# A 128-step gated recurrence on one core: where the three gate sums are joined, and the order of VectorE's side work around place 7

## The reference, cut to what matters

```python
def step(h, inp):
    x_t, prop = inp
    comb = jnp.concatenate([x_t, h], axis=-1)
    z = jax.nn.sigmoid(comb @ Wz + bz)
    r = jax.nn.sigmoid(comb @ Wr + br)
    comb2 = jnp.concatenate([x_t, r * h], axis=-1)
    h_cand = jnp.tanh(comb2 @ Wh + bh)
    h_new = (1.0 - z) * h + z * h_cand
    h_next = jnp.where(prop, jnp.tanh(h_new @ Wp + bp), h_new)
    return (h_next, h_new)
# do_prop: every 4th step except the last; result: x + the h_new of all steps
```

## Time and profile before

| | busy us | share of the span | instructions |
|---|---|---|---|
| TensorE matmuls (PE) | 1033.4 | 99% | 20746 |
| weight loads (PEld) | 953.2 | 92% | 20746 |
| VectorE (DVE) | 880.9 | 85% | 2880 |
| ScalarE (ACT) | 777.0 | 75% | 1789 |

### The profile page before, as it was taken

One profiled execution on the slowest core, in us unless ns is written; L12 is line 12 of the kernel. 1 busy time (PEld: TensorE's weight loads), 2 busy tenths in 40 slices (PEclk: granted clock), 3 DMA queues, 4 the chain that ended last, 5 costly groups with the idle time before them and its releaser, 6 DMA issues.

```text
span 1038.9 us, 48087 instructions
## 1 busy us (share of the span) xinstructions
PE 1033.4 (99%) x20746; PEld 953.2 (92%) x20746; DVE 880.9 (85%) x2880; ACT 777.0 (75%) x1789; POOL 0.2 (0%) x4
## 2 busy tenths in 40 slices
PE   9999999999999999999999999999999999999998
PEld 4577999999999999999999999999999999999998
DVE  6978888898989899898989989989898998876666
ACT  6877777777878778777887777878777777665565
POOL 0000000000000000000000000000000000000000
PEclk9999999999999999999999999999999999999999
DMA  9312211001111011110011110111100100000001
GB/s 331 110 43 84 84 54 44 23 23 43 43 43 43 4 44 42 44 43 23 23 44 43 44 43 11 35 44 43 44 29 17 43 23 23 23 10 17 24 24 44
DMA packets 38484, 47.26 MB, mean 45 GB/s; under 512 B 2176, under 2 KB 34048, under 8 KB 37888
## 3 DMA queue, kind: packets, MB, share of 16 engines
q1 hardware_dynamic: 38000, 44.12, 12.6%
q10 hardware_dynamic: 272, 0.07, 0.0%
HBM read 27.40 MB, written 16.78 MB: 43 GB/s over the span
## 4 chain that ended last, share of the span: by engine, by line
PE 98%; DMA 1%; SPq 0%; DVE 0%; issue 0%; ACT 0%; DVEq 0%
PE acc L1360 38%; PE x_acc L1274 34%; PE acc L1368 17%; PE x_acc L1164 8%; DMA x_part<-wz_dram 1%; PE x_acc L1295 0%; SPq L419 0%; SPq L416 0%; DVE mag_win L982 0%; SPq L425 0%; SPq L424 0%; DVE x_lo L889 0%; PE acc L1170 0%; ACT gate L745 0%; DVE new L1099 0%
## 5 line engine op out<-in xcount | busy, mean ns | idle before, releaser
L1274 PE MATMUL x_acc<-x_hi,win_hi 128*128 128x256 f16 x1092 | 298.0, 273 | 0.0
L1274 PE MATMUL x_acc<-x_lo,win_hi 128*128 128x256 f16 x1092 | 297.9, 273 | 0.0
L1274 PE MATMUL x_acc<-x_hi,win_lo 128*128 128x256 f16 x1092 | 297.9, 273 | 0.0
L589 ACT ACTIVATE gate<-gate,unscale 128x128 f32<-128x128 f32 (+1 forms) x316 | 128.6, 432 | 136.4 <-DVE gate L1067 77.7
L595 ACT ACTIVATE gate<-acc,unscale 128x128 f32<-128x128 f32 (+1 forms) x384 | 123.8, 371 | 97.9 <-PE acc L1360 97.7
L1368 PE MATMUL acc<-h_split,wrec_hi 128*128 128x128 f16 x2704 | 178.8, 220 | 0.0
L1360 PE MATMUL acc<-h_split,wrec_lo 128*128 128x64 f16 x4096 | 177.5, 194 | 0.0
L1360 PE MATMUL acc<-q_split,wrec_hi 128*128 128x64 f16 x4000 | 162.2, 194 | 0.0
L555 ACT ACTIVATE x_part<-x_acc,bias,part_unscale 128x256 f32<-128x256 f32 x312 | 154.6, 561 | 6.4 <-PE x_acc L1274 5.5
L1360 PEld LDWEIGHTS acc<-h_split,wrec_lo 128*128 128x128 f16 x4096 | 154.2, 98 | 4.7
L1368 PEld LDWEIGHTS acc<-h_split,wrec_hi 128*128 128x128 f16 x2704 | 153.7, 98 | 0.0
(11 more groups left out here) (141 smaller groups left out, 1517.5 us busy)
## 6 DMA issues: line engine op xcount, KB each, us to landing
out_dram<-x_blk SPq DMA_DIRECT2D x30, 512.0 KB, 3.2
x_blk<-x_dram SPq DMA_DIRECT2D x24, 512.0 KB, 3.8
x_blk<-x_dram SPq DMA_DIRECT2D x3, 1024.0 KB, 8.7
x_part<-wz_dram SPq DMA_DIRECT2D x4, 256.0 KB, 6.8
x_part<-wh_dram SPq DMA_DIRECT2D x4, 256.0 KB, 6.6
x_part<-wr_dram SPq DMA_DIRECT2D x1, 1024.0 KB, 10.9
x_part<-wz_dram SPq DMA_DIRECT2D x1, 1024.0 KB, 13.1
x_part<-wh_dram SPq DMA_DIRECT2D x1, 1024.0 KB, 15.3
```

Source lines behind the costliest of these rows:

```text
L589: nc.scalar.activation(gate[g][:, half], gate[g][:, half], func, scale=unscale[:, g:g + 1]).then_inc(gate_ready[g], 1)
L1274: mm = nc.tensor.matmul(in_halves(x_acc[bank][:])[:, j], weights[g][:, slot_w, k, j * P:(j + 1) * P], in_halves(values[m % 2][:, slot_x, : ...
```

## The change

R becomes joint in every step from 16 to 110 (`JOINT_RESET`), so in steps 16, 17, 18, 109, 110 and at place 7 of steps 23 to 103 too: 16 steps more. C becomes joint in steps 17 and 110 too. Z stays as it is. In these 16 steps four matmuls of the place's stages now stand ahead of C, in steps 17 and 110 four more inside C. Seed Z of step 16 moves behind the propagation's tanh. On VectorE, stage 17 is ended no longer at place 6 but at the very end of place 7 (`END_BEHIND_PROPAGATION`); stage 19 is ended ahead of, not behind, adding state 7; and where Z is joint at place 6, states 4 to 6 are added at the end of place 6 instead of the end of place 7 (`STATES_AHEAD_AT`). Steps 14, 15 and 110, 111 are outside that last rule: there the 768 columns stay at the end of place 7.

```diff
--- before.py
+++ after.py
@@ -33,8 +33,8 @@
 AHEAD = 32
 REC_SUM_AT = 4
 EARLY_PROP_SHARE = 1.4
-JOINT_RESET_AT = (0, 1, 2, 3, 4, 5, 6)
 AHEAD_OF_C = 4
+JOINT_RESET = range(16, 111)
 JOINT = range(19, 109)
 JOINT_CANDIDATE_AT = (1, 4, 6)
 WITHIN_C = 4
@@ -55,6 +55,9 @@
          (2, 1), (2, 2), (1, 7), (2, 3), (2, 5), (2, 4), (2, 6), (2, 7)]
 
 STAGES_AT = [((), (0, 1)), ((), (2, 3, 4)), ((), (5, 6)), ((7, 8), (9,)), ((), (10, 11, 12)), ((), (13, 14)), ((), (15, 16, 17)), ((18, 19), (20,))]
+ENDS_AT = [(), (4,), (5,), (), (11, 12), (), (), (19,)]
+END_BEHIND_PROPAGATION = 17
+STATES_AHEAD_AT = 6
 
 SLOT_AT = {2: (5, 6, 6, 7, 8, 9, 10), 3: (4, 5, 6, 7, 7, 8, 9)}
 SLOT_AT_LATER = (1, 2, 3, 4, 5, 6, 7)
@@ -373,15 +376,19 @@
 
         def behind_propagation(t):
 
-            return propagates(t) and joint(t) and joint(t + 1)
+            return propagates(t) and t + 1 in JOINT_RESET
 
         def joint_reset(t):
 
-            return joint(t) and t % BLOCK in JOINT_RESET_AT
+            return t in JOINT_RESET
 
         def joint_candidate(t):
 
-            return joint(t) and t % BLOCK in JOINT_CANDIDATE_AT
+            return t in JOINT_RESET and t % BLOCK in JOINT_CANDIDATE_AT
+
+        def states_ahead(t):
+
+            return joint(t) and t % BLOCK == STATES_AHEAD_AT
 
         def resets_before(t):
             return sum(joint_reset(step) for step in range(t))
@@ -1075,7 +1082,7 @@
 
                 if t == 1:
                     make_scale(PROP)
-                if t == JOINT[0] - 2:
+                if t == JOINT_RESET[0] - 2:
                     nc.vector.tensor_scalar(half_seed_scale[:], seed_scale[:, R:C + 1], 0.5, None, ALU.mult).then_inc(half_seed_scale_ready, 1)
 
                 if joint_candidate(t):
@@ -1122,6 +1129,13 @@
                     dve.wait_ge(hi, count + n + 1)
                     dve.wait_ge(h_new_ready, 2 * t + n + 1)
                     subtract_hi(h_out, split, half).then_inc(lo, 1)
+                ends = ENDS_AT[s] if m + 1 in SEVEN else ()
+                if prop:
+                    for n in ends:
+                        end_quarter(m + 1, n)
+                if states_ahead(t):
+                    dve.wait_ge(h_new_ready, 2 * t + 2)
+                    add_states(t + 2 - CHUNK, t + 1)
                 if prop or t >= T - CHUNK:
                     dve.wait_ge(h_new_ready, 2 * t + 2)
                     add_states(t, t + 1)
@@ -1136,8 +1150,8 @@
                 if m + 2 == LAST:
                     for k in SPLIT_AT.get(s, ()):
                         split_x(m + 2, k)
-                for n in stages_of(t)[0] + stages_of(t)[1]:
-                    if ORDER[n][1] in (5, 6):
+                if not prop:
+                    for n in ends:
                         end_quarter(m + 1, n)
                 if t in (1, 2):
                     split_rec(PROP, t - 1)
@@ -1153,7 +1167,10 @@
                         dve.wait_ge(h_hi_ready, 2 * t + n + 3)
                         dve.wait_ge(h_prop_ready, 2 * props + n + 3)
                         subtract_hi(h_prop, h_split, half).then_inc(h_lo_ready, 1)
-                    add_states(t + 1 - CHUNK, t)
+                    if not states_ahead(t - 1):
+                        add_states(t + 1 - CHUNK, t)
+                    if s == BLOCK - 1 and m + 1 in SEVEN:
+                        end_quarter(m + 1, END_BEHIND_PROPAGATION)
 
         @block.tensor
         def _(pe):
@@ -1409,8 +1426,6 @@
                 if joint(t):
                     rec(Z, wrec_lo, h_split, HIGH, 0)
                     rec_both(Z, h_split, range(KC)).then_inc(product_done[Z], 1)
-                    if joint_reset(t):
-                        stage(m + 1, (stages_first + stages_last)[0], stop=AHEAD_OF_C)
                 else:
                     rec(Z, wrec_hi, h_split, LOW, 0)
                     rec(Z, wrec_lo, h_split, HIGH, 0)
@@ -1420,6 +1435,8 @@
                     if not behind:
                         rec(Z, wrec_hi, h_split, HIGH[1:], 1).then_inc(product_done[Z], 1)
 
+                if joint_reset(t):
+                    stage(m + 1, (stages_first + stages_last)[0], stop=AHEAD_OF_C)
                 if t == 1:
                     reduce_magnitude(PROP)
                 if t == 0:
```

## The result

| | median us | lowest to highest | runs |
|---|---|---|---|
| before | 1040.54 | 1039.50 to 1041.61 | 19 |
| after | 1042.39 | 1041.38 to 1043.64 | 19 |

The ratio is 1.0019 with a 95% interval of 1.0013 to 1.0026: 1.9 us slower, clear of zero, and on the edge of the 0.2% that counts as a difference here. The forecast was 1042.1.

What follows compares the result with a forecast made beforehand. TensorE streams while everybody else waits for it, so only its matmuls or new waits count. Outer steps +1.8, place 7 +0.44, joins -0.8 sum to +1.45 us: 1042.1 us against the median of 1040.63, range 1039.6 to 1044.0.

Steps and rivals of the forecast that it cites:

- A join saves 0.045 us: TensorE: each newly joint gate replaces 32 matmuls of 64 columns by 16 of 128; eighteen joins give 0.8 us less.
- The busy time per instruction: Rival: TensorE's joined pairs save 20 ns each, 5.9 us over 288 pairs, giving 1034.8 us; chance 0.03.
- The spare of 0.03: In a joint step, `q` starts 0.47 us ahead of its use and needs 0.44, leaving 0.03 us spare.
- the 0.05 of plain-Z steps: Steps 16, 17, 18, 109, 110: 0.07 us less cover between R and `q`, so 0.05 us lost in each.
- Step 16, 0.44: States and stage 17 stand ahead of R's sum on VectorE, making it late by 0.39; 0.44 us lost.
- Step 109, 0.2: VectorE ends two quarters at 908.98, R's sum is wanted at 908.82; late by 0.16, 0.2 us lost.
- Steps 110 and 111, 0.5 and 0.6: Sigmoids come late on ScalarE behind splits, seeds and a later tanh; 0.5 us more in step 110, 0.6 in 111.
- Place 7: Eleven steps, 23 to 103: R's sum hidden by 0.8 us, stage 20 loses 0.04 in each, 0.44 us in all.
- the tail at P + 7.38: VectorE's work from R's sum to behind the state at place 7 ends 7.38 us after step start P, 0.53 later.
- The covers hold: Rival: ScalarE and VectorE close up, no wait opens, only the joins' 0.8 us saving shows: 1039.8 us; chance 0.17.
- Slower by stage 20: Rival: stage 20 waits for stage 19 at each place 7, 1.1 us per 0.1 us of later tail: 1043.9; chance 0.17.
- stage 17's end would stand ahead of R's sum: Rival: side work stays in the way, R's sum 0.5 us late at every place 7: +5.5 us, 1047; chance 0.03.

Runs made afterwards that it cites:

- ahead5: Changed kernel with five stage matmuls instead of four ahead of C where R is joint and Z plain (16, 17, 18, 109, 110); one time of 1041.46 us.
- states14: Changed kernel with states 12 to 14 added at the end of step 14 instead of step 15; one time of 1041.42 us.
- split_first: Changed kernel with the last block's four x splits one place later each: two at place 6, two at place 7 of block 13; one time of 1042.19 us.
- split_late: Changed kernel with the last two splits of the last block's x at place 7 of block 13 instead of place 6; 1042.43 us, ratio 1.0016.
- stage19_last: Changed kernel with stage 19 ended behind the addition of state 7 again; 1046.58 us, ratio 1.0059.
- stage17_at6: Changed kernel with stage 17 ended at place 6 and states 4 to 6 added at the end of place 7 again; 1047.81 us, ratio 1.0071.
- outer_off: Changed kernel with R joint only in steps 19 to 108, place 7 still joint; 1040.74 us, ratio 1.0003 to the kernel before.

## Why the prediction was right, point by point

- **A join saves 0.045 us, no more.** Right in kind, a little too large. The matmul counts moved as said. By the unrounded starts, R's first product to C's first takes 2.760 us in a plain place 7 and 3.157 in a joint one, of which four stage matmuls are 4 x 0.1092: the join saves 0.04, eighteen of them 0.7 us and not 0.8. The busy time per instruction would have said 5.9 us less, and nothing of it came. The matmuls of 128 columns cost after what they cost before. The 81 ns that the Trainium skill gives for one in a stream ("TensorE: Matmul & The Clock Gate", section "Back-to-back issue gap") did not show; the trace disagrees with 56 ns from start to start.
- **The spare of 0.03 and the 0.05 of plain-Z steps.** Right: 0.05 in steps 17 and 18, 0 with one stage matmul more (ahead5).
- **Step 16, 0.44.** Measured 0.44, the cause shown by states14.
- **Step 109, 0.2.** Measured 0.19. That VectorE's two quarters cause it was only read from R's sum following them at once. More cover helps (ahead5); the quarters themselves were not moved.
- **Steps 110 and 111, 0.5 and 0.6 on top of the 0.09 of before.** Measured 0.59 in all and 0.61; split_first and split_late show ScalarE's splits as what stands ahead. The terms of the working, tanh and seeds later, were not measured one by one.
- **Place 7.** R's sum covered, the tail at P + 7.38 (measured 485.79 - 478.42 = 7.37), stage 20 waiting 0.04: right, and stage19_last shows that it is a wait with a price of eleven. Only the 0.01 lost in the matmul behind the wait was missing.
- **The sum.** Forecast +1.45, medians +1.85. The traces, by the table +1.9, show where the difference of 0.4 lies. The outer steps cost 1.57 with their seven joins taken off (0.61 - 0.21 for the pause of step 21, and 1.17); the forecast had 1.84 - 7 x 0.045 = 1.52. The eleven places 7 cost 0.13, where the forecast had 0.44 - 11 x 0.045 = -0.06: the joins were 0.005 too large and the waits 0.01 too small, eleven times. And the pauses of VectorE took 0.75 us from TensorE in place of 0.57, +0.18, a term that the forecast doesn't have. Together that is 1.9. That these leftovers are small is partly luck: where the pauses fall was not worked out, and in other kernels here they cost from 0.2 to 1.5 us.
- **The rivals.** "The covers hold" fell with the losses at steps 16 and 109 to 111. "Slower by stage 20" names a real mechanism and its price, but the tail was not late by more than 0.04; moving the state's addition behind stage 19 is what kept it off. Its price, the 0.2 us of step 47, came from a pause of VectorE (last section), not from a late tail. That stage 17's end would stand ahead of R's sum was excluded by the diff, and stage17_at6 shows that it costs 0.37 a step.

## What to carry to other kernels

Where an engine streams at 99%, price a change by start-to-start distances and then measure the spare of each of its waits from a place where it truly waited; the table of waits hid eleven waits of 0.04, and busy time per instruction was wrong by a factor of eight. Lengthening a chain that has 0.03 us to spare is safe only in the steps whose side work is known: check the steps at the edges of a range, where two exceptions meet, one by one. Work that is moved away from one wait has to be followed on every engine that takes part in it, as the splits showed, whose VectorE halves ate most of what ScalarE had regained; and work taken out of idle time, as the slot's split, gives nothing and can open a wait where it lands.

## What the runs showed of the hardware that was not expected

VectorE pauses now and then for up to about a quarter of a microsecond with no other engine to wait for, and what it works on comes that much later. VectorE and then TensorE of the changed kernel, step 68:

```profile
585.34 0.48 DVE L1063 TENSOR_TENSOR q_full<-gate,h_prop 128x128 f32<-128x128 f32 x2
586.08 0.49 DVE L1039 TENSOR_TENSOR q_split<-q_full,q_split 128x128 f16<-128x128 f32 x2 [0.26 <-DVE q_full L1063]
```
```profile
586.06 0.27 PE L1291 MATMUL x_acc<-x_lo,win_hi 128*128 128x256 f16 x1
586.43 0.56 PE L1385 MATMUL acc<-q_split,wrec_hi 128*128 128x128 f16 x7
```

TensorE's next matmul comes 0.37 us after the last instead of 0.11: the pause goes straight through to TensorE. The kernel before has such pauses too: the 0.2 us of step 47 that the earlier trace rows show began with a pause of 0.25 in VectorE, put down to issue. The profiled execution of the changed kernel has three such losses in TensorE of 0.20 to 0.26 us and one of 0.05 in the steps from 19 to 108, the kernel before has one of 0.21, two of 0.14 and one of 0.06.

They look irregular in time, but they are not irregular in the program. Number VectorE's records in the trace from 0, those of its waits included (3764 in the changed kernel). From step 19 on, every pause of more than 0.06 us that no other engine ended stands in the changed kernel at one of the numbers 703, 831, 1599, 1983, 2111, 2367, 2623 and 2751, and each is 63 more than a multiple of 128. In all eleven traces there are 90 such pauses, and every one stands at 63 or 64 more than a multiple of 128; not every such number has a pause. The five kernels with the same number of records in VectorE's queue as the changed one, itself among them, have their pauses at the same eight. In step 21 all nine kernels in which steps 16 to 18 are joint have one at 703 or 704, `q` lo, here of the changed kernel:

```profile
214.11 0.28 DVE L1039 TENSOR_TENSOR q_split<-q_full,q_split 128x128 f16<-128x128 f32 x1
214.65 0.29 DVE L1039 TENSOR_TENSOR q_split<-q_full,q_split 128x128 f16<-128x128 f32 x1 [0.25 <-issue]
```

The kernel before and outer_off, whose queues number otherwise there, have no loss in step 21; there number 703 is the first instruction of state hi, 2.3 us later in the step. So an instruction added early in VectorE's queue moves every later pause to another operation, and whether it costs anything depends on the spare of the operation that it hits: that is how a change in steps 16 to 18 costs 0.2 us in step 21. What the engine does at every 128th record was not tried.
